# Rotation of the conditioning states: who forms the sums, and in which order the scans and products stand

## The chip, the cores and the metric

One core of a Trainium2 chip runs the whole kernel. The metric is the device time of one execution in microseconds (us). The kernel before took 882.53 us (median of 3 runs, 880.73 to 883.51). The engines are TensorE (PE, matrix products), VectorE (DVE), ScalarE (ACT), GpSimd (POOL) and SyncE (SP, which only issues transfers here). They run side by side and wait for one another by semaphores.

## The reference

The kernel is a small vision tower: patch embedding, a gated linear attention layer with a conditioning branch, a quantised feed-forward layer, softmax attention and a mixture of experts. The change touches only the conditioning branch of the first attention layer. There a projection `p` of the normalised tokens, 128 wide, is taken as 64 pairs, and each pair runs through a recurrence over the 37 tokens of a sequence: the state is turned by a fixed angle and the new pair is added.

```python
p2 = jnp.moveaxis(p.reshape(b, s, bw // 2, 2), 1, 0)
c, sn = (jnp.cos(rot_theta), jnp.sin(rot_theta))
def rot_step(carry, xt):
    s0, s1 = (carry[..., 0], carry[..., 1])
    new = jnp.stack([c * s0 - sn * s1 + xt[..., 0], sn * s0 + c * s1 + xt[..., 1]], axis=-1)
    return (new, new)
_, states = jax.lax.scan(rot_step, init, p2)
cond = _rmsnorm(jnp.moveaxis(states, 0, 1).reshape(b, s, bw), cond_norm_w)
deltas = cond @ delta_W
```

The deltas are then added to the query, key and value projections.

## The kernel before

There are 32 sequences of 37 tokens, 1184 columns in all (`T`), with the features on the 128 partitions. Most stages work in four parts of 296 columns (`CH`); the rotation works in two halves of 592.

The recurrence is computed without a step per token. A state that is turned back by its token's angle obeys a plain running sum. So for each half the kernel does the following (lines 1413 to 1429, VectorE only). It multiplies the two projections (one with even and odd swapped), which lie in PSUM, by tables of cosines and sines: four products, `r1`, `r2`, `r3`, `rp`, for each half. It adds them in pairs (L1423, L1424). It forms two running sums along the tokens with `tensor_tensor_scan` (L1425, L1426), whose first operand `keep_mask` is 0 at the first token of each sequence and 1 elsewhere. It multiplies the running sums by the tables again (L1427, L1428) and adds the two products (L1429); the result in `r1` is the state. After the four products of both halves, the first half goes through all of its seven instructions before the second half starts.

Each finished half increments the semaphore `states`. ScalarE waits for it and squares the half into `rp` (L1101), which increments `csq`. TensorE averages the squares over the partitions with two small products per half (L1891). Between the halves its program has a fixed number of filler products, `keep_clock(fill(("cr", 0)), KEEP["csq"])` with `KEEP["csq"]` = 36 (L1796); they compute nothing that is used, and keep TensorE busy. Then ScalarE takes the square root (L1104), VectorE the reciprocal (L1434), TensorE spreads it over the partitions (L1897), and VectorE scales the states (L1438) and splits them into two halves of precision (L1441). TensorE needs these for the projections that follow.

Before these, TensorE computes the gate projections, whose last product ends while VectorE is in the second half. GpSimd builds constants and masks at the very start (event `masks`) and then waits for the end of this branch (`chl`, L984), after which it builds the decay tables (L991, L995).

Each engine's order is written by hand. `link` increments an engine's own semaphore and, unless `hold=False`, waits for it, so that the next instruction may read what this one wrote. `after(eng, key)` waits until a PSUM bank has been emptied.

Of the kernel before, what the change touches and what calls it, by code (L numbers as in the profile page):

```python
# [7 lines left out]
ALU = mybir.AluOpType  # L8
# [9 lines left out]
NCH = 4  # L18
BC = B // NCH
CH = BC * S  # L20
# [21 lines left out]
for _n, _w in [("cb", 6), ("cw", 24), ("gb", 2), ("dbb", 1), ("opb", 2), ("fcw", 24), ("fcb", 8), ("bq", 2),  # L42
# [16 lines left out]
    + ["wlinh", "wlinl", "xth", "xtl", "condh", "condl", "ctrlh", "ctrll", "dwh", "dwl", "wouth", "woutl", "wqkh",  # L59
       "wqkl", "gwh", "gwl"]  # L60

    + [f"ln{i}_{k}" for i in range(1, 5) for k in ("sq", "rec", "xh", "xl")]

    + ["states", "csq", "crec", "chh", "chl", "dbh", "dbl"]

    + ["conv", "post", "qksq", "qkrec", "kqh", "kql", "vh", "vl"]

# [192 lines left out]
def tower(nc, a, out, probe=None):  # L260
    place = plan_tiles()
    order = list(place)
    with ExitStack() as ctx:
        def sb(name, shape, dt=F32):
            return ctx.enter_context(nc.sbuf_tensor(name, shape, dt))

        def sem(name):
            return ctx.enter_context(nc.semaphore(name))

        ev = {name: sem(name) for name in EVENTS}  # L270
        own = {e: sem("own_" + e) for e in ("act", "dve", "pool")}
# [17 lines left out]
        def who(key):  # L289
            return place[key][1]  # L290

        def nth(key):
            return place[key][2]

        def full(eng, key):

            eng.wait_ge(filled[who(key)], nth(key))
# [3 lines left out]
        xh = sb("xh", [128, 2, TP], F16)  # L301
        xl = sb("xl", [128, 2, TP], F16)
# [14 lines left out]
        def carve(at, *shape, dt=F32, parts=128):  # L317
            n = int(np.prod(shape))
            words = n if dt == F32 else (n + 1) // 2
            assert at + words <= ARENA, (at, words)  # L320
            v = arena[0:parts, at:at + words]
            if dt != F32:
                v = v.bitcast(dt)
            names = "abcde"[:len(shape)]
            return v.rearrange(f"p ({' '.join(names)}) -> p {' '.join(names)}",
                               **{k: s for k, s in zip(names[1:], shape[1:])}) if len(shape) > 1 else v
# [4 lines left out]
        def after(eng, key):  # L331

            eng.wait_ge(emptied[who(key)], nth(key))

        def cols(q, n=CH):
            return slice(q * n, (q + 1) * n)
# [15 lines left out]
        sq = carve(LN_AT + 2368, 2, T)  # L352
# [14 lines left out]
        rp = carve(24640, T)  # L367
        rs_ = carve(25824, T)
        r1 = carve(27008, T)
        r2 = carve(28192, T)  # L370
        r3 = carve(29376, T)
        keep_mask = carve(30560, T)
# [5 lines left out]
        chh = carve(32020, T, dt=F16)  # L378
        chl = carve(32612, T, dt=F16)
# [9 lines left out]
        dbh = carve(13024, T, dt=F16, parts=32)  # L389
        dbl = carve(13616, T, dt=F16, parts=32)  # L390
# [393 lines left out]
        def moe_pe(pe, product, keep_clock):  # L784
# [60 lines left out]
            def rows_out(hf):  # L845
                for n in range(3):
                    pe.wait_ge(ev["summed"], 4 * hf + (2, 4, 4)[n])
                    for t, _, m in half_tiles(0)[2 * n:2 * n + 2]:
                        for c in range(2):
                            at = (t % 2) * D + 128 * c  # L850
                            ins = pe.transpose(banks[ACC[n]][0:m, at:at + 128],
                                               hT[:, c, hf * HALF + 128 * t:hf * HALF + 128 * t + m], ident[:])
                    ins.then_inc(ev["outT"], 1)
# [80 lines left out]
        def _(pool):  # L934
            chain = [0]
# [45 lines left out]
            link(pool.memset(xh[:, :, T:TP], 0.0))  # L981
            pool.memset(xl[:, :, T:TP], 0.0).then_inc(ev["masks"], 1)

            pool.wait_ge(ev["chl"], NCH)  # L984
            pool.wait_ge(ev["dwl"], 1)
            after(pool, ("dbT",))
# [61 lines left out]
        def _(act):  # L1048
            chain = [0]
# [47 lines left out]
                                           bias=sm("gb", c)).then_inc(emptied["act"], 1)  # L1097
            act.activation(warm[:, 4:5], eps[:, 0:1], ACT.Sqrt)
            for h in range(2):
                act.wait_ge(ev["states"], h + 1)  # L1100
                act.activation(rp[:, cols(h, 2 * CH)], r1[:, cols(h, 2 * CH)], ACT.Square).then_inc(ev["csq"], 1)  # L1101
            full(act, ("cv",))

# [69 lines left out]
            for s_ in range(S):  # L1173
# [4 lines left out]
                if WQ_AT <= s_ < WQ_AT + 6:  # L1178
                    i, kind = (s_ - WQ_AT) % 2, (s_ - WQ_AT) // 2
# [122 lines left out]
        def _(dve):  # L1302
            chain = [0]

            def link(ins, hold=True):

                chain[0] += 1
                ins.then_inc(own["dve"], 1)
                if hold:
                    dve.wait_ge(own["dve"], chain[0])  # L1310
# [78 lines left out]
            def small_inputs():  # L1389
# [12 lines left out]
            cosb, sinpb, sinnb = (x.unsqueeze(1).unsqueeze(1).to_broadcast([128, 2, BC, S])  # L1402
                                  for x in (trig[:, 0], sinp, sinn))

            def half(x, h):
                return x[:, cols(h, 2 * CH)].rearrange("p (i b s) -> p i b s", i=2, s=S)

            def pair(i, h):
                b0 = place[("p", i, 2 * h)][0] % 8
                full(dve, ("p", i, 2 * h + 1))  # L1410
                return psum[:, b0:b0 + 2, 0:CH].rearrange("p i (b s) -> p i b s", s=S)

            for h in range(2):
                link(dve.tensor_tensor(half(r1, h), pair(0, h), cosb, ALU.mult), hold=False)
                dve.tensor_tensor(half(r2, h), pair(0, h), sinnb, ALU.mult).then_inc(emptied["dve"], 2)
                link(dve.tensor_tensor(half(r3, h), pair(1, h), sinpb, ALU.mult), hold=False)
                dve.tensor_tensor(half(rp, h), pair(1, h), cosb, ALU.mult).then_inc(emptied["dve"], 2)
            after(dve, ("p", 1, NCH - 1))
            dve.wait_ge(own["dve"], chain[0])
            dve.wait_ge(ev["masks"], 1)  # L1420
            for h in range(2):
                t = cols(h, 2 * CH)
                link(dve.tensor_tensor(r1[:, t], r1[:, t], r3[:, t], ALU.add), hold=False)  # L1423
                link(dve.tensor_tensor(r2[:, t], r2[:, t], rp[:, t], ALU.add))  # L1424
                link(dve.tensor_tensor_scan(r3[:, t], keep_mask[:, t], r1[:, t], 0.0, ALU.mult, ALU.add), hold=False)  # L1425
                link(dve.tensor_tensor_scan(rs_[:, t], keep_mask[:, t], r2[:, t], 0.0, ALU.mult, ALU.add))  # L1426
                link(dve.tensor_tensor(half(r1, h), half(r3, h), cosb, ALU.mult), hold=False)  # L1427
                link(dve.tensor_tensor(half(r2, h), half(rs_, h), sinnb, ALU.mult))  # L1428
                dve.tensor_tensor(r1[:, t], r1[:, t], r2[:, t], ALU.add).then_inc(ev["states"], 1)  # L1429
            dve.wait_ge(ev["states"], 2)  # L1430
            dve.wait_ge(ev["dwh"], 1)
            dve.tensor_tensor(dwl, delta_raw, dwh, ALU.subtract).then_inc(ev["dwl"], 1)
            after(dve, ("cv",))
# [107 lines left out]
            def reduce_o(t):  # L1541
# [3 lines left out]
                                  AX, ALU.add).then_inc(ev["o"], 1)  # L1545

            added_after = [added_by(s_, hi - 1) for s_ in range(S) for _, hi in later_ops(s_)]
            n_ = 0
            for s_ in range(S):
# [137 lines left out]
            for n in range(3):  # L1687
                t = slice(512 * n, min(512 * n + 512, T))
# [89 lines left out]
        def _(pe):  # L1778
# [166 lines left out]
            for key in AORDER:  # L1945
                ps = fill(key)
                if key[0] == "A":
                    _, j, c, n_ = key
                    if (j, c, n_) == (0, 0, 0):
                        keep_clock(ps, KEEP["km"])  # L1950
                    pe.wait_ge(ev["km"], 2 * j + c + 1)
                    for i in range(ASPLIT[n_]):
                        b = ASTART[n_] + i
                        ins = product(ps[0:74, 74 * i:74 * i + 74], kqh[:, c, b].rearrange("p i s -> p (i s)"),
                                      kql[:, c, b].rearrange("p i s -> p (i s)"),
                                      KM[:, c, b].rearrange("p i s -> p (i s)"),
                                      KML[:, c, b].rearrange("p i s -> p (i s)"), True, True)
                else:
                    _, j, n_ = key
                    after(pe, ("A", j, 1, len(ASPLIT) - 1))  # L1960
                    s0, ns = at_group(n_)
                    for x in range(ns):
                        ins = pe.transpose(ps[:, 74 * x:74 * x + 74], ASB[:, j % 2, s0 + x, :], ident[0:74, 0:74])  # L1963
                ins.then_inc(filled[who(key)], 1)
# [317 lines left out]
```

## Time and profile before

| | |
|---|---|
| median of 3 runs | 882.53 us (880.73 to 883.51) |
| profiled execution | 881.1 us, of which 879.4 us are its span |
| TensorE products busy | 793.7 us (90%) |
| VectorE busy | 614.7 us (70%) |
| ScalarE busy | 391.3 us (45%) |
| GpSimd busy | 183.5 us (21%) |
| mean granted clock of TensorE | 0.977 |

The profile is of one execution. The span goes from the first to the last instruction; the time around it is 1.7 us. Busy shares are over the whole span, and a stage can have another limit than the whole. Times in the rows below are us from the start of the span.

### The profile page before, as it was taken

To read this page: it belongs to the slowest core of one execution; us is meant where nothing else is said; L and a number is where in the kernel's file an instruction comes from. 1 tells how busy PE (TensorE), PEld (TensorE's weight loads), DVE (VectorE), ACT (ScalarE), POOL (GpSimd) and SP (SyncE) were. 2 spreads that over 40 slices of the span, in tenths; PEclk is the share of its full clock that TensorE was granted. 3 is DMA by queue.
4 is the path that set the end of the run, shared out by engine and by line. 5 is a ranking of instruction groups with operands and counts; after the bars stand their busy time and mean duration, and the time that the engine had idled before them with its cause. 6 is when DMAs were issued, how large, how long until landed. Compare 5 with 4: busy or idle time off the path is not lost.

```text
span 879.4 us, 19821 instructions
## 1 busy us (share of the span) xinstructions
PE 793.7 (90%) x7700; PEld 586.2 (67%) x7700; DVE 614.7 (70%) x976; ACT 391.3 (45%) x561; POOL 183.5 (21%) x197
## 2 busy tenths in 40 slices
PE   4998978989986988977798998799999999999997
PEld 3665757944543666755487885477777777777775
DVE  5796697678787386898767977767777655545544
ACT  5344764610224143666457965334444432323332
POOL 7000790006999801000402420000000000000000
PEclk9999979999999999999999999799999999999999
DMA  8000000020000000010130001144444322222221
GB/s 310 1 2 1 3 1 3 3 96 1 0 0 1 0 2 1 1 39 1 37 78 14 22 21 38 57 127 158 154 150 154 109 68 57 70 69 69 68 61 51
DMA packets 24073, 46.07 MB, mean 52 GB/s; under 512 B 2605, under 2 KB 10541, under 8 KB 23629
## 3 DMA queue, kind: packets, MB, share of 16 engines
q1 hardware_dynamic: 24013, 45.21, 16.8%
q8 instruction: 45, 0.74, 0.4%
q14 instruction: 15, 0.12, 0.0%
HBM read 41.91 MB, written 1.36 MB: 49 GB/s over the span
## 4 chain that ended last, share of the span: by engine, by line
PE 70%; DVE 21%; ACT 4%; issue 3%; POOL 1%; DMA 1%; SPq 0%; DVEq 0%; ACTq 0%; POOLq 0%
PE psum L1790 11%; PE psum L1791 11%; PE psum L1792 11%; PE psum L1982 6%; PE psum L1992 4%; PE psum L828 4%; PE psum L829 4%; PE psum L830 4%; PE psum L2124 1%; DVE arena L1460 1%; PE psum L2170 1%; DVE arena L1658 1%; PE psum L1963 1%; PE psum L2187 1%; PE psum L2156 1%
## 5 line engine op out<-in xcount | busy, mean ns | idle before, releaser
L1790 PE MATMUL psum<-xh,arena 128*128 128x296 f16 (+1 forms) x664 | 193.3, 291 | 8.3 <-DVE xl L1333 5.0
L1791 PE MATMUL psum<-xl,arena 128*128 128x296 f16 (+1 forms) x664 | 193.2, 291 | 0.0
L1792 PE MATMUL psum<-xh,arena 128*128 128x296 f16 (+1 forms) x664 | 193.2, 291 | 0.0
L697 DVE TENSOR_TENSOR arena<-arena 128x592 f16<-128x592 f32 x68 | 52.7, 775 | 61.1 <-ACT arena L608 60.8
L603 ACT ACTIVATE arena<-psum 128x592 f32<-128x592 f32 x66 | 43.8, 664 | 115.7 <-PE psum L1792 115.7
L1790 PEld LDWEIGHTS psum<-xh,arena 128*128 (+2 forms) x664 | 65.3, 98 | 30.8 <-DVE xl L1333 4.5
L752 DVE TENSOR_TENSOR arena<-psum,arena 128x592 f32<-128x592 f32 x64 | 49.6, 775 | 50.8 <-PE psum L1792 50.6
L828 PE MATMUL psum<-arena 128*128 128x296 f16 x272 | 79.9, 294 | 4.6 <-DVE arena L697 3.8
L608 ACT ACTIVATE arena<-arena 128x592 f16<-128x592 f32 x66 | 46.0, 696 | 77.6 <-DVE arena L691 74.8
L829 PE MATMUL psum<-arena 128*128 128x296 f16 x272 | 79.9, 294 | 0.0
L830 PE MATMUL psum<-arena 128*128 128x296 f16 x272 | 79.8, 293 | 0.0
L1982 PE MATMUL psum<-arena 128*128 128x512 f32 (+1 forms) x160 | 65.8, 550 | 14.2 <-DVE arena L527 14.2
L1792 PEld LDWEIGHTS psum<-xh,arena 128*128 (+2 forms) x664 | 65.4, 98 | 19.1
L1791 PEld LDWEIGHTS psum<-xl,arena 128*128 (+2 forms) x664 | 65.3, 98 | 18.3
L1790 PE MATMUL psum<-arena 128*74 128x74 f16 (+3 forms) x348 | 58.3, 229 | 18.6 <-DVE arena L1343 12.9
L1982 PEld LDWEIGHTS psum<-arena 128*128 128x128 f32 x160 | 30.3, 195 | 46.5 <-issue 28.4
L527 DVE TENSOR_TENSOR arena<-arena,psum 128x320 f32<-128x320 f32 (+7 forms) x67 | 53.9, 805 | 8.4 <-PE psum L1982 8.4
L1012 POOL TENSOR_TENSOR arena<-arena 128x64 f32<-128x64 f32 (+23 forms) x24 | 43.6, 1819 | 72.4 <-ACT arena L1175 55.3
L691 DVE TENSOR_TENSOR arena<-arena 128x592 f32<-128x592 f32 x68 | 52.7, 775 | 8.4 <-ACT arena L603 1.5
L1791 PE MATMUL psum<-arena 128*74 128x74 f16 (+3 forms) x348 | 58.4, 229 | 0.0
L1792 PE MATMUL psum<-arena 128*74 128x74 f16 (+3 forms) x348 | 58.3, 230 | 0.0
L1175 ACT ACTIVATE arena<-arena 128x64 f32<-128x64 f32 x37 | 11.7, 316 | 97.7 <-DVE arena L1560 97.6
(321 smaller groups left out, 1675.3 us busy)
## 6 DMA issues: line engine op xcount, KB each, us to landing
arena<-comb SPq DMA_DIRECT2D x62, 296.0 KB, 3.3
arena<-in_wmoe SPq DMA_DIRECT2D x34, 384.0 KB, 3.0
arena<-in_xt SPq DMA_DIRECT2D x4, 864.0 KB, 9.6
arena<-in_w SPq DMA_DIRECT2D x2, 1024.0 KB, 6.6
arena<-arena SPq DMA_DIRECT2D x6, 187.0 KB
arena<-in_ctrl SPq DMA_DIRECT2D x1, 1056.0 KB, 9.1
out<-arena SPq DMA_DIRECT2D x2, 512.0 KB, 3.1
arena<-in_wlin SPq DMA_DIRECT2D x1, 768.0 KB, 4.4
```

The costliest lines, as they stand in the source:

```text
L527: return eng.tensor_tensor(dst[:, 0:w * HJ * DH].rearrange("p (t j v) -> p t j v", j=HJ, v=DH), a_, u, ALU.mult)
L608: act.activation(ah[:, s_], t1, ACT.Copy).then_inc(ev["ah"], 1)
L691: dve.tensor_tensor(t1, t1, sg, ALU.mult).then_inc(ev["a"], 1)
L697: dve.tensor_tensor(al[:, s_], t1, ah[:, s_], ALU.subtract).then_inc(ev["al"], 1)
L752: dve.tensor_tensor(t1v, up, cb_[:, s_].rearrange("p (c t) -> p c t", c=2), ALU.mult).then_inc(ev["t1"], 1)
L828: pe.matmul(dst, high, ah[:, s_, cols(ch)], start=start, stop=False, skip_group_check=True)
L829: pe.matmul(dst, high, al[:, s_, cols(ch)], start=False, stop=False, skip_group_check=True)
L830: ins = pe.matmul(dst, low, ah[:, s_, cols(ch)], start=False, stop=stop, skip_group_check=True)
L1790: pe.matmul(dst, wh, mh, start=start, stop=False)
L1791: pe.matmul(dst, wh, ml, start=False, stop=False)
L1792: return pe.matmul(dst, wl, mh, start=False, stop=stop)
L1982: pe.matmul(row(g0, g1 - g0), negident, ring[:, n_ % RING, 64 * (g0 - base):64 * (g1 - base)], start=False, stop=s_ + 1 == g0, skip_group_ ...
```

## The change

The six sums of the rotation were all VectorE's. Now GpSimd forms five: four before the scans, and the one that finishes the first half. The one that finishes the second half stays on VectorE. VectorE's order becomes: the eight products from PSUM, the four scans of both halves, then the products back of the first half and of the second. Two semaphores carry this: `rotated`, incremented by VectorE's products, and `rotated_sum`, incremented by GpSimd's sums. ScalarE's first square waits for GpSimd's fifth sum, its second for the only increment of `states`. Two semaphores of another stage that nothing used are gone. TensorE's program, with its 36 fillers, is as before.

```diff
+            for h in range(2):
+                t = cols(h, 2 * CH)
+                pool.wait_ge(ev["rotated"], 2 * h + 2)
+                after(pool, ("p", 1, 2 * h + 1))
+                pool.tensor_tensor(r1[:, t], r1[:, t], r3[:, t], ALU.add).then_inc(ev["rotated_sum"], 1)
+                pool.tensor_tensor(r2[:, t], r2[:, t], rp[:, t], ALU.add).then_inc(ev["rotated_sum"], 1)
+            pool.wait_ge(ev["rotated"], 6)
+            pool.tensor_tensor(r1[:, cols(0, 2 * CH)], r1[:, cols(0, 2 * CH)], r2[:, cols(0, 2 * CH)], ALU.add).then_inc(
+                ev["rotated_sum"], 1)
...
             for h in range(2):
-                act.wait_ge(ev["states"], h + 1)
+                act.wait_ge(*((ev["states"], 1) if h else (ev["rotated_sum"], 5)))
                 act.activation(rp[:, cols(h, 2 * CH)], r1[:, cols(h, 2 * CH)], ACT.Square).then_inc(ev["csq"], 1)
...
             for h in range(2):
-                link(dve.tensor_tensor(half(r1, h), pair(0, h), cosb, ALU.mult), hold=False)
+                dve.tensor_tensor(half(r1, h), pair(0, h), cosb, ALU.mult).then_inc(ev["rotated"], 1)
                 dve.tensor_tensor(half(r2, h), pair(0, h), sinnb, ALU.mult).then_inc(emptied["dve"], 2)
-                link(dve.tensor_tensor(half(r3, h), pair(1, h), sinpb, ALU.mult), hold=False)
+                dve.tensor_tensor(half(r3, h), pair(1, h), sinpb, ALU.mult).then_inc(ev["rotated"], 1)
                 dve.tensor_tensor(half(rp, h), pair(1, h), cosb, ALU.mult).then_inc(emptied["dve"], 2)
-            after(dve, ("p", 1, NCH - 1))
-            dve.wait_ge(own["dve"], chain[0])
             dve.wait_ge(ev["masks"], 1)
             for h in range(2):
                 t = cols(h, 2 * CH)
-                link(dve.tensor_tensor(r1[:, t], r1[:, t], r3[:, t], ALU.add), hold=False)
-                link(dve.tensor_tensor(r2[:, t], r2[:, t], rp[:, t], ALU.add))
+                dve.wait_ge(ev["rotated_sum"], 2 * h + 1)
                 link(dve.tensor_tensor_scan(r3[:, t], keep_mask[:, t], r1[:, t], 0.0, ALU.mult, ALU.add), hold=False)
-                link(dve.tensor_tensor_scan(rs_[:, t], keep_mask[:, t], r2[:, t], 0.0, ALU.mult, ALU.add))
-                link(dve.tensor_tensor(half(r1, h), half(r3, h), cosb, ALU.mult), hold=False)
-                link(dve.tensor_tensor(half(r2, h), half(rs_, h), sinnb, ALU.mult))
-                dve.tensor_tensor(r1[:, t], r1[:, t], r2[:, t], ALU.add).then_inc(ev["states"], 1)
-            dve.wait_ge(ev["states"], 2)
+                dve.wait_ge(ev["rotated_sum"], 2 * h + 2)
+                link(dve.tensor_tensor_scan(rs_[:, t], keep_mask[:, t], r2[:, t], 0.0, ALU.mult, ALU.add), hold=False)
+            dve.wait_ge(own["dve"], chain[0])
+            for h in range(2):
+                t = cols(h, 2 * CH)
+                dve.tensor_tensor(half(r1, h), half(r3, h), cosb, ALU.mult).then_inc(ev["rotated"], 1)
+                dve.tensor_tensor(half(r2, h), half(rs_, h), sinnb, ALU.mult).then_inc(ev["rotated"], 1)
+                if h:
+                    dve.wait_ge(ev["rotated"], 8)
+                    dve.tensor_tensor(r1[:, t], r1[:, t], r2[:, t], ALU.add).then_inc(ev["states"], 1)
+            dve.wait_ge(ev["rotated_sum"], 5)
+            dve.wait_ge(ev["states"], 1)
```

## Rows read from the trace of the kernel before

**Rows 1.** The page: shares of the chain that ended last, by engine.
```profile
PE 70%; DVE 21%; ACT 4%; issue 3%; POOL 1%; DMA 1%; SPq 0%; DVEq 0%; ACTq 0%; POOLq 0%
```

**Rows 2.** The chain of waits from 52 us: start, duration, engine and line.
```profile
52.28 0.79 DVE arena L1416
...
66.66 0.70 ACT arena L1101
67.41 0.72 PE psum L1891 x4
```

**Rows 3.** VectorE's timeline, 50 to 67: start, duration, line, operation, shapes.
```profile
50.08 0.76 DVE L1417 TENSOR_TENSOR arena<-psum,arena 128x592 f32<-128x592 f32 x1
50.77 0.76 DVE L1414 TENSOR_TENSOR arena<-psum,arena 128x592 f32<-128x592 f32 x1
...
52.98 0.76 DVE L1417 TENSOR_TENSOR arena<-psum,arena 128x592 f32<-128x592 f32 x1
53.77 0.78 DVE L1423 TENSOR_TENSOR arena<-arena 128x592 f32<-128x592 f32 x1
...
55.27 1.39 DVE L1425 TENSOR_TENSOR_SCAN arena<-arena 128x592 f32<-128x592 f32 x1
56.58 1.36 DVE L1426 TENSOR_TENSOR_SCAN arena<-arena 128x592 f32<-128x592 f32 x1
...
65.85 0.77 DVE L1429 TENSOR_TENSOR arena<-arena 128x592 f32<-128x592 f32 x1
```

**Rows 4.** ScalarE's timeline at 60 us; in brackets the idle before and its releaser.
```profile
60.28 0.70 ACT L1101 ACTIVATE arena<-arena 128x592 f32<-128x592 f32 x1 [0.69 <-DVE arena L1429]
```

**Rows 5.** TensorE's timeline, 60 to 68 us.
```profile
60.26 0.29 PE L1792 MATMUL psum<-xh,arena 128*128 128x296 f16 x1
61.12 0.69 PE L1891 MATMUL psum<-arena,mean_ones 128*32 128x296 f32 x4 [0.57 <-ACT arena L1101]
61.75 4.82 PE L1796 MATMUL psum<-arena 128*128 128x296 bf16 x36
67.41 0.69 PE L1891 MATMUL psum<-arena,mean_ones 128*32 128x296 f32 x4 [0.84 <-ACT arena L1101]
```

**Rows 6.** GpSimd's groups, shapes apart: busy us and mean ns, then idle before.
```profile
L1043 POOL TENSOR_TENSOR arena<-arena 101x592 f16<-101x592 f32 x16 | 20.3, 1268 | 66.2 <-ACT arena L1292 66.2
...
L995 POOL TENSOR_TENSOR arena<-arena 128x444 f32<-128x444 f32 x4 | 3.7, 932 | 0.0
...
L1012 POOL TENSOR_TENSOR arena<-arena 128x640 f32<-128x640 f32 x1 | 1.5, 1529 | 0.0
...
L527 POOL TENSOR_TENSOR arena<-arena 128x576 f32<-128x576 f32 x1 | 1.2, 1216 | 0.0
```

**Rows 7.** GpSimd's timeline, 121 to 126 us.
```profile
121.98 0.48 POOL L995 TENSOR_TENSOR arena<-arena 128x169 f32<-128x169 f32 x1
...
123.08 0.94 POOL L995 TENSOR_TENSOR arena<-arena 128x444 f32<-128x444 f32 x1
124.09 1.51 POOL L995 TENSOR_TENSOR arena<-arena 128x169 f32<-128x169 f32 x1
```

**Rows 8.** VectorE's timeline, 120 to 126 us.
```profile
120.29 1.32 DVE L1473 TENSOR_TENSOR arena<-arena 128x1184 f16<-128x1184 f32 x1
...
122.65 0.45 DVE L1488 TENSOR_TENSOR arena<-arena,psum 128x296 f32<-128x296 f32 x1
123.13 2.13 DVE L1473 TENSOR_TENSOR arena<-arena 128x1184 f16<-128x1184 f32 x1
```

**Rows 9.** TensorE: an idle in its timeline; stretches (length, busy, granted clock, DMA).
```profile
188.70 1.99 PE L1982 MATMUL psum<-arena 128*128 128x512 f32 x3 [3.65 <-DVE arena L527]
...
73.50:73.60 0.10, 0.10 (x2) 0.88 0.00 0
76.90:77.00 0.10, 0.10 (x2) 0.56 0.00 0
189.60:189.70 0.10, 0.10 (x2) 0.64 0.00 0
193.00:193.10 0.10, 0.10 (x2) 0.80 0.00 0
```

More of the change, by code:

```diff
@@ L60 @@
        "wqkl", "gwh", "gwl"]
-    + [f"ln{i}_{k}" for i in range(1, 5) for k in ("sq", "rec", "xh", "xl")]
-    + ["states", "csq", "crec", "chh", "chl", "dbh", "dbl"]
+    + [f"ln{i}_{k}" for i in range(1, 5) for k in (("sq", "rec") if i == 2 else ("sq", "rec", "xh", "xl"))]
+    + ["rotated", "rotated_sum", "states", "csq", "crec", "chh", "chl", "dbh", "dbl"]
     + ["conv", "post", "qksq", "qkrec", "kqh", "kql", "vh", "vl"]
```

## The prediction

> **What bounds the kernel now.** I read the chain of waits first. TensorE has 70% of the chain and VectorE 21% [rows 1], but a share over the whole span does not price this edit; the stage does. In the stage of the rotation the chain is all VectorE, from the product at 52.28 us to the end of the last sum; then it goes through ScalarE's square at 66.66 and TensorE's small products at 67.41 [rows 2]. VectorE's timeline gives the durations there [rows 3]: pieces of 592 columns take 0.76 to 0.78 us, and start 0.69 us apart with no wait between them (50.08, 50.77) or 0.79 with one (52.98, 53.77); a scan takes 1.39 or 1.36 us and the next starts after 1.31.
>
> TensorE's timeline [rows 5] is the view that decides. Its last gate product ends at 60.26 + 0.29 = 60.55. The squares of the first half come from ScalarE at 60.28 + 0.70 = 60.98 [rows 4], its products of the first half start at 61.12, and behind them in its queue stand 36 filler products that keep its clock, written in the program between the two halves: 61.75 to 66.57. The second half starts at 67.41, after an idle of 0.84. So today the fillers fit between the halves, because the first half's states are ready 6.4 us before the second's. They are not conditional: whenever the first half starts, the second cannot start before 0.63 + 4.82 us have passed, plus the little gap that a change of product costs, in all about 5.5.
>
> **The change part by part.** VectorE loses five of six sums, nominally 5 x 0.69 to 0.79, or some 3.7 us. The order also changes: all four scans now come before any product back, and the sum that finishes the first half is GpSimd's fifth. Call the four scans S1 to S4 (first half S1, S2), GpSimd's sums P1 to P5, the products back Q1 to Q4.
>
> P1 and P2. GpSimd has had nothing to do since its masks were done. Its wait ends with the last product of the first half, 50.08 + 0.76 = 50.84. No row has a dense sum of 592 in f32 on GpSimd; the nearest are 444 elements at 0.93 us, 576 at 1.216, 592 with f16 out at 1.268, and 640 in another line at 1.529 [rows 6]. I take 1.25, nearest to the 576 and the 592, and keep 0.95 and 1.5 as ends. P1 and P2 run 50.9 to 53.4, beside VectorE's products that read PSUM and one table. That costs nothing: a GpSimd piece of 169 elements beside VectorE's PSUM products takes 0.48 [rows 7], and those keep their 0.45 [rows 8]. If that cover were wrong, S1 would start up to 1.2 us late.
>
> S1 to S4 with P3 and P4. Here the two engines are not independent. At 123.08 GpSimd starts a piece of 0.94, ending 124.02; VectorE's piece with two SBUF inputs starts at 123.13 and takes 2.13 us, against 1.32 for the same shape at 120.29. It ends at 125.26, 1.24 after GpSimd let go. The next GpSimd piece, 169 elements, starts at 124.09 and takes 1.51 instead of 0.48: it ends at 125.60, 0.34 after VectorE [rows 7, 8]. So each waits for the whole of the other's instruction; a waiting VectorE piece then needs its duration less 0.08, a waiting GpSimd piece its duration less 0.14. A scan reads two SBUF tensors (the keep mask and the sums), as does a product back. No row shows a scan beside GpSimd: the bounds are no conflict, and the full one. I take the full one.
>
> The Trainium skill, GPSIMD Engine Reference, Key points, says that GpSimd shares its SBUF interfaces with VectorE and contends with VectorE instructions that have two SBUF inputs. A scan has two, so by that rule it belongs with the piece at 123.13, and the sum below stands; without it the sum would be the smaller one that I give as a rival.
>
> The sum, with conflict. S1 starts at 52.98 + 0.69 = 53.67 and has the port; P3 may start only at 53.8, when the last PSUM product is done, and waits. S1 ends 55.03; P3 ends 55.03 + 1.11 = 56.14; S2 ends 56.14 + 1.28 = 57.42; P4 ends 58.53; S3 ends 59.81; S4 follows with nothing of GpSimd's in between and ends 61.1. (If GpSimd did not get in between S1 and S2, S3 would have to wait for P3 instead, and the total would be the same.) Q1 and Q2 end at 61.15 + 0.69 + 0.76 = 62.6. P5 needs Q2, but Q3 is already running until 63.3, so P5 ends at 63.3 + 1.11 = 64.4. ScalarE's square: 64.43 to 65.13. TensorE starts the first half 0.14 later, as it does now [rows 4, 5], at 65.27; its fillers run 65.90 to 70.72; the second half starts at 70.74. Before: 67.41. That is **+3.3 us**. VectorE meanwhile ends Q4 at 65.1 and the last sum at 65.9; the second half's squares are there at 66.6, four microseconds before they are wanted. So the states are done slightly earlier than now (65.9 against 65.85 + 0.78 = 66.6 [rows 3]), and it buys nothing: what is late next is the filler queue. P3, P4 and P5 each carry the GpSimd price, so its ends move the sum by -0.9 and +0.8.
>
> The clock. TensorE would idle from 60.55 to 65.27, 4.7 us, where it now idles 0.57. After its idle of 3.65 us at 188.70 the granted clock fell from 2.4 to 1.2 GHz at 189.63 and came back at 193.04 [rows 9]: the granted shares in the edge slices (0.64 and 0.80) place the two edges. Those 3.4 us at the lower level cost 1.7 us of work. A spell like that at about 65 would fall into the fillers, which take twice as long in it. Bounds: 0, and 3.4 for two spells in a row; I take **+1.7**.
>
> The rest moves as a block. The square root, the reciprocal, the row broadcast and TensorE's projections hang on the second half and shift with it. VectorE's subtraction for the delta weights still hides under the squares. The two removed semaphores and the two new ones have no instruction of cost. Nothing downstream starts without this chain, so nothing absorbs the shift.
>
> The sum is 3.3 + 1.7 = 5.0 us. The profiled execution took 881.1 us (span 879.4); that gives 886.1. The median of the three runs is 882.53, 1.4 above the profiled one, so the forecast on its scale is 887.5.
>
> **The rivals.** (a) Conflict, but no extra clock spell, or one later spell less: the change costs 3.3, 885.8. For it: shorter idles at this stage leave the clock alone. Against: the idle becomes eight times as long.
>
> (b) Scans and GpSimd do not conflict. S4 ends at 53.67 + 3 x 1.31 + 1.36 = 58.96, Q2 at 60.4, P5 at 61.75, the squares at 62.5, TensorE starts at 62.6 and the second half at 68.1: +0.7, 883.2; with a clock spell +2.4, 884.9. For it: no row shows a scan beside GpSimd. Against: the piece at 123.13.
>
> (c) Not slower. The mechanism: as (b), and the fillers, which then run without the present gap of 0.84 before the second half, spare TensorE the clock spell that now begins at 73.58 and ends at 76.99 (edge slices 0.88 and 0.56 [rows 9]), just as it needs its rate for the projections. That gives back 1.7: -1.0, 881.5. It decides in favour as soon as the first half reaches TensorE before 61.95 (67.41 less 5.46), or before 63.6 if the spell goes. With the conflict it comes at 65.3, so even without that spell the sum is above zero. To beat 0.3% it would need the fillers gone from between the halves, and they are not.
>
> **How the numbers follow.** Forecast 0.45 (4.1 to 5.9 us by the GpSimd price; 886.6 to 888.5), (a) 0.25, (b) 0.16, (c) 0.08, other clock spells in stages that start 5 us later 0.06. A difference within 0.3%, 2.65 us either way, cannot be told from none here. All of the forecast, 0.20 of (a) and 0.05 of (b) and the rest lie above it: slower 0.70. Faster needs (c) with a second spell gone: 0.03. Same 0.27. The range must reach (b) at 883.2 and stop above the forecast with half a spell and a dear GpSimd more: 882.8 to 890.2.
>
> **What would show it.** Right: GpSimd's third and fourth sums take over 2 us each, or the scans do; the fourth scan ends near 61; TensorE idles over 4 us from 60.5; the first half's products start near 65.3 and the second's come straight behind the 36 fillers with no wait for ScalarE; ScalarE's second square ends well before. A granted clock of 1.2 GHz within the fillers shows the last term. Wrong: scans 1.31 apart beside GpSimd's sums (then (b)); a GpSimd sum far from 1.25 us in P1 and P2; a wait for the squares behind the fillers, which would mean that the second half and not the filler queue is late.

## The result: slower by 0.7%, and the profile after

The changed kernel took 889.29 us in the median of 7 runs (884.88 to 892.63), the kernel before 882.89 us beside it. The ratio is 1.007, with a 95% interval of 1.0046 to 1.0093: 4 to 8 us slower. In a second set (12 runs) the medians were 887.18 and 883.39 us and the ratio 1.0059 (1.0031 to 1.0087). A ratio is worked out from all runs of both kernels and need not be that of the two medians, so both are given below. The profiled execution took 884.88 us, the fastest of the first seven, so its span of 883.2 us shows less than the median does; the stage itself has to be read in the trace.

The shares of the chain are nearly those of [rows 1]: TensorE 70%, VectorE 20% for 21%, GpSimd 2% for 1%.

VectorE's timeline of the changed kernel, to be read against [rows 3]. The last product from PSUM starts at 52.96, as before (52.98):

```profile
53.64 1.44 DVE L1432 TENSOR_TENSOR_SCAN arena<-arena 128x592 f32<-128x592 f32 x1
55.01 2.55 DVE L1434 TENSOR_TENSOR_SCAN arena<-arena 128x592 f32<-128x592 f32 x1
57.48 2.56 DVE L1432 TENSOR_TENSOR_SCAN arena<-arena 128x592 f32<-128x592 f32 x1
59.96 1.36 DVE L1434 TENSOR_TENSOR_SCAN arena<-arena 128x592 f32<-128x592 f32 x1
61.36 0.77 DVE L1438 TENSOR_TENSOR arena<-arena 128x592 f32<-128x592 f32 x1
...
62.73 0.77 DVE L1438 TENSOR_TENSOR arena<-arena 128x592 f32<-128x592 f32 x1
63.42 2.00 DVE L1439 TENSOR_TENSOR arena<-arena 128x592 f32<-128x592 f32 x1
65.45 0.78 DVE L1442 TENSOR_TENSOR arena<-arena 128x592 f32<-128x592 f32 x1
```

GpSimd's timeline, the five sums:

```profile
50.98 1.45 POOL L988 TENSOR_TENSOR arena<-arena 128x592 f32<-128x592 f32 x1 [31.22 <-DVE arena L1427]
52.39 1.44 POOL L989 TENSOR_TENSOR arena<-arena 128x592 f32<-128x592 f32 x1
53.87 2.45 POOL L988 TENSOR_TENSOR arena<-arena 128x592 f32<-128x592 f32 x1
56.27 2.52 POOL L989 TENSOR_TENSOR arena<-arena 128x592 f32<-128x592 f32 x1
62.90 1.89 POOL L991 TENSOR_TENSOR arena<-arena 128x592 f32<-128x592 f32 x1 [4.10 <-DVE arena L1439]
```

The two views interlock: GpSimd and VectorE take turns. Whichever engine is at work is said to have the port, as in the prediction; no run looks behind that word. The first scan has the port until about 55.1; the third sum, issued at 53.87, ends at 56.32. The second scan, alone 1.36, takes 2.55; the fourth sum waits for it and ends at 58.79; and the third scan takes 2.56. The same happens with the fifth sum (1.89) and the last product back (2.00 in place of 0.77). Beside the products from PSUM a sum takes 1.45.

ScalarE's squares, against [rows 4], and TensorE's timeline, against [rows 5]:

```profile
64.82 0.70 ACT L1111 ACTIVATE arena<-arena 128x592 f32<-128x592 f32 x1 [5.25 <-POOL arena L991]
66.27 0.70 ACT L1111 ACTIVATE arena<-arena 128x592 f32<-128x592 f32 x1 [0.75 <-DVE arena L1442]
```
```profile
60.24 0.29 PE L1806 MATMUL psum<-xh,arena 128*128 128x296 f16 x1
65.66 1.20 PE L1905 MATMUL psum<-arena,mean_ones 128*32 128x296 f32 x4 [5.13 <-ACT arena L1111]
66.80 6.44 PE L1810 MATMUL psum<-arena 128*128 128x296 bf16 x36
73.17 0.69 PE L1905 MATMUL psum<-arena,mean_ones 128*32 128x296 f32 x4
```

The second half's squares are there at 66.97. TensorE uses them at 73.17, because the 36 fillers stand in front, and it reached these late and at the low clock. Before, that row was at 67.41. The chain, which in [rows 2] went from VectorE through ScalarE's second square to TensorE, now passes through the fillers:

```profile
64.82 0.71 ACT arena L1111
65.53 0.14 issue
65.66 1.20 PE psum L1905 x4
66.87 6.37 PE psum L1810 x36
73.24 0.65 PE psum L1905 x4
```

The granted clock at the two edges of the low spell (stretch; length, busy, granted clock, DMA), against [rows 9]:

```profile
63.30:63.40 0.10, 0.00 (x0) 0.98 0.00 0
...
70.20:70.30 0.10, 0.10 (x2) 0.88 0.00 0
```

It falls to 1.2 GHz at 63.4, 2.9 us into the idle that began at 60.53, and returns to 2.4 GHz at 70.2. That is 6.8 us, twice the 3.4 us of the spell at 189.63 in [rows 9]. TensorE had work in 4.5 us of it, which costs 2.3 us.

Executions differ by up to 1.6 us in when this stage begins, so from here on I measure the second half from the start of the last product from PSUM: before 67.41 - 52.98 = 14.43 us, changed 73.17 - 52.96 = 20.21, a loss of 5.8.

GpSimd's first clear of the decay tables comes 6.7 us later than before; the attention weights' turn at 391 us only 3.7 later. The rows of the kernel before:

```profile
92.39 0.36 POOL L988 MEMSET arena<- 128x148 f32 x1 [72.51 <-ACT arena L1124]
...
391.39 2.39 PE L2032 MATMUL psum<-ident,arena 128*128 128x128 f32 x10 [3.88 <-DVE arena L1658]
```

and of the changed kernel:

```profile
99.05 0.36 POOL L998 MEMSET arena<- 128x148 f32 x1 [34.26 <-ACT arena L1134]
...
395.13 2.40 PE L2046 MATMUL psum<-ident,arena 128*128 128x128 f32 x10 [3.88 <-DVE arena L1672]
```

In between the kernel before has the low spell at 189.63 to 193.04 [rows 9], and the changed kernel's profile has none there: 1.7 of the 3 us. It has one from 315.9 to 319.4 that the kernel before lacks. So what is left of a delay at the end of one execution also hangs on where such spells fall; whether that is a rule in the times is taken up below.

### The profile page after: what moved, and what is told of

Read it like the earlier page. It is cut to its first block, busy times and chain, and to the rows that moved or that the text cites. A ratio compares the mean times of both kernels' runs of the same rounds, so it can differ in the third digit from the quotient of the medians.

```text
span 883.2 us, 19823 instructions
## 1 busy us (share of the span) xinstructions
PE 797.3 (90%) x7700; PEld 588.3 (67%) x7700; DVE 615.3 (70%) x971; ACT 391.2 (44%) x561; POOL 192.7 (22%) x202
## 3 DMA queue, kind: packets, MB, share of 16 engines
HBM read 41.91 MB, written 1.36 MB: 49 GB/s over the span
## 4 chain that ended last, share of the span: by engine, by line
PE 70%; DVE 20%; ACT 4%; issue 3%; POOL 2%; DMA 1%; SPq 0%; DVEq 0%; ACTq 0%; POOLq 0%
PE psum L1804 11%; PE psum L1805 11%; PE psum L1806 11%; PE psum L1996 6%; PE psum L2006 4%; PE psum L828 4%; PE psum L829 4%; PE psum L830 4%; PE psum L2138 1%; DVE arena L1474 1%; PE psum L2184 1%; DVE arena L1672 1%; PE psum L1977 1%; PE psum L2201 1%; PE psum L2170 1%
## 5 line engine op out<-in xcount | busy, mean ns | idle before, releaser
L697 DVE TENSOR_TENSOR arena<-arena 128x592 f16<-128x592 f32 x68 | 52.7, 775 | 61.1 <-ACT arena L608 60.9
L1996 PE MATMUL psum<-arena 128*128 128x512 f32 (+1 forms) x160 | 63.9, 537 | 12.5 <-DVE arena L527 12.5
L1804 PEld LDWEIGHTS psum<-arena 128*74 128x74 f16 (+2 forms) x348 | 38.4, 116 | 23.2 <-issue 14.8
```

Source lines behind the costliest of these rows:

```text
L697: dve.tensor_tensor(al[:, s_], t1, ah[:, s_], ALU.subtract).then_inc(ev["al"], 1)
L1804: pe.matmul(dst, wh, mh, start=start, stop=False)
L1996: pe.matmul(row(g0, g1 - g0), negident, ring[:, n_ % RING, 64 * (g0 - base):64 * (g1 - base)], start=False, stop=s_ + 1 == g0, skip_group_ ...
```

## The experiments

Theory: three terms. The port and the new order delay the first half; the fillers, which stand behind the first half in TensorE's queue, then delay the second; the idle before them costs the clock. Rivals: GpSimd or the new order is slow in itself; all of it is the clock; all of it is the queue.

**The fillers in front of the first half.** In TensorE's program of the changed kernel:

```diff
-                if q == 2:
+                if q == 0:
                     keep_clock(fill(("cr", 0)), KEEP["csq"])
```

> The changed kernel with its 36 fillers moved from between the halves to in front of the first half's products on TensorE. Theory (the fillers stand behind a first half that now comes late, and the idle of 5 us costs the clock): the fillers run at 60.6 to 65.4 at 2.4 GHz, the first half's products start near 65.7, the second's near 67.1 (before: 67.41, changed kernel: 73.17), no spell of 1.2 GHz at 63 to 71; the time is within 1.5 us of the kernel before, some 6 under the changed one. Rival (the sums on GpSimd and the new order on VectorE themselves make it slow): the second half's products stay near 73 or the time stays 4 us or more above the kernel before.

Measured: 882.87 us against 883.3, ratio 1.0002 (0.9977 to 1.0028). TensorE's timeline:

```profile
61.27 4.81 PE L1810 MATMUL psum<-arena 128*128 128x296 bf16 x36
66.48 0.69 PE L1905 MATMUL psum<-arena,mean_ones 128*32 128x296 f32 x4 [0.40 <-ACT arena L1111]
67.92 0.69 PE L1905 MATMUL psum<-arena,mean_ones 128*32 128x296 f32 x4 [0.75 <-ACT arena L1111]
```

This execution ran 0.9 us late from the start (last product at 53.86): the second half is at 14.06, 0.37 under the kernel before, and it waits for ScalarE again. With GpSimd's five sums, the stretched scans and the new order all kept, the whole loss is gone. What the change cost came through the place of the fillers; what it gained in the stage was 0.4 us.

**No fillers between the halves** (the changed kernel with `"csq": 0` for 36).

> The changed kernel with no fillers at all between the halves (36 to 0). Theory: the first half starts at 65.7 as in the changed kernel, after the same idle of 5.1 us and with the clock at 1.2 GHz, the second near 67.1; the 16 fillers and the small products behind it run at the low clock, so it pays 1 to 2 us of the clock but not the 4.8 of the fillers: 1 to 3 us above the kernel before. Rival: the fillers' only effect is on the clock and without them later stages lose more than 5 us: no better than the changed kernel.

Measured: 885.08 us against 883.3, ratio 1.002 (0.9998 to 1.0042), +1.8 us. (One run of the twelve took 2751 us, and why is not known. The median counts it and would be 884.82 without it; the ratio leaves it out.) TensorE's timeline:

```profile
66.49 1.20 PE L1905 MATMUL psum<-arena,mean_ones 128*32 128x296 f32 x4 [5.13 <-ACT arena L1111]
67.94 1.20 PE L1905 MATMUL psum<-arena,mean_ones 128*32 128x296 f32 x4 [0.24 <-ACT arena L1111]
69.07 3.64 PE L1810 MATMUL psum<-arena 128*128 128x296 bf16 x16
```

The second half starts on time (67.94 - 53.79 = 14.15), but at 1.2 GHz: its products take 1.20 for 0.69 and the 16 fillers behind them 3.64 for 2.24. The size is as expected, though the interval's lower end touches no change.

**Fillers in both places.** The changed kernel with `if q in (0, 2):`, 72 fillers in all.

> The changed kernel with 36 fillers in front of the first half as well, those between the halves kept. It parts the queue from the clock: the theory says that the clock stays at 2.4 GHz from 60 to 71, the first half's products start where they do in the changed kernel, and the second's 0.63 + 4.84 later, that is 3.6 us after the place of the kernel before (14.43 us after the last product from PSUM; here 18.0) and 2.1 us earlier than in the changed kernel (20.2). Time: +3 to +4 us against the kernel before. Rival (all of the loss is the clock): back to the kernel before, 14.4. Rival (all of it is the queue): no better than the changed kernel, 20.2.

Measured: 887.84 us against 883.39, ratio 1.0044 (1.0024 to 1.0064), +3.9 us. TensorE's timeline:

```profile
60.47 4.81 PE L1810 MATMUL psum<-arena 128*128 128x296 bf16 x36
65.68 0.69 PE L1905 MATMUL psum<-arena,mean_ones 128*32 128x296 f32 x4 [0.40 <-ACT arena L1111]
66.31 4.82 PE L1810 MATMUL psum<-arena 128*128 128x296 bf16 x36
71.06 0.69 PE L1905 MATMUL psum<-arena,mean_ones 128*32 128x296 f32 x4
```

The second half is at 71.06 - 53.06 = 18.0, as expected to the tenth. So of the 5.8 us, 3.6 are the queue and 2.2 the clock. Both rivals that name one cause fall by the place of the second half; the times alone (2.1 to 5.7 us here, 2.7 to 7.7 for the changed kernel in the same set) would not part this kernel from the changed one.

**More fillers in the kernel before:** 66, and after that 96, in place of 36 (`"csq": 66`, `"csq": 96`). Its sums, scans and order are untouched.

> The kernel before with 66 fillers between the halves in place of 36, nothing else. Theory: the queue of fillers is what the second half waits for once it is longer than the gap between the halves: 30 x 0.134 = 4.0 us more, less the idle of 0.84 that is there: second half at 70.6 in place of 67.41, time +3.2 us. Rival (the fillers pay for themselves by the clock): less than +1.5 us.

> The kernel before with 96 fillers between the halves in place of 36. The dose of 66 gave a second half 3.0 us late but a time only +0.2% (0 to 0.47%), too near to both readings. Theory: 60 x 0.134 less 0.84 = 7.2 us late at the second half, and the time follows: +5.5 to +8 us. Rival (later stages absorb a delay of this stage, through the clock or otherwise): second half 7.2 late, time under +4.

The rows of the second half, first with 66, then with 96:

```profile
70.09 0.69 PE L1891 MATMUL psum<-arena,mean_ones 128*32 128x296 f32 x4
```
```profile
74.54 0.69 PE L1891 MATMUL psum<-arena,mean_ones 128*32 128x296 f32 x4
```

With 66 it starts 17.4 after the last product (3.0 late), with 96 21.3 (6.9 late). The times: with 66, 883.99 us against 883.3, ratio 1.0023 (1.0 to 1.0047), that is +2.0 us (0 to 4.1); with 96, 891.69 against 883.39, ratio 1.0093 (1.0061 to 1.0126), +8.2 us. In the trace the first dose does what the theory says, but its time does not tell the readings apart: the medians differ by 0.7 us, which is what the rival expected, and the ratio lies between the two. The second dose does: a delay of 6.9 us in this stage is not absorbed later.

**Four more GpSimd sums in the kernel before.** They read the keep mask and write to a spare place; nothing uses them. (The wait that lets the last two start also stands on VectorE, which costs its first scan 0.1 us.)

```diff
+            for x in range(4):
+                if x == 0:
+                    after(pool, ("p", 1, 1))
+                elif x == 2:
+                    pool.wait_ge(ev["extra_go"], 1)
+                pool.tensor_tensor(spare[:, x], keep_mask[:, cols(0, 2 * CH)], keep_mask[:, cols(1, 2 * CH)],
+                                   ALU.add).then_inc(ev["extra"], 1)
```

> The kernel before, its own sums all on VectorE, with four GpSimd sums of 128x592 more whose output nothing reads: two start beside VectorE's products from PSUM, two beside the first half's scans. Theory (a VectorE instruction with two SBUF inputs and a GpSimd sum exclude each other, products from PSUM do not): the first two take 1.45 us and the products keep 0.76; the last two take about 2.5, the scan beside them 2.5 in place of 1.36, and the states of both halves come some 2.4 us later. Rival (in the changed kernel the scans were late by their waits on the sums, not by the port): all four take 1.45 and both scans keep 1.36 to 1.44.

GpSimd's timeline and then VectorE's:

```profile
51.17 1.44 POOL L990 TENSOR_TENSOR arena<-arena 128x592 f32<-128x592 f32 x1 [31.41 <-DVE arena L1426]
52.57 1.46 POOL L990 TENSOR_TENSOR arena<-arena 128x592 f32<-128x592 f32 x1
55.55 1.44 POOL L990 TENSOR_TENSOR arena<-arena 128x592 f32<-128x592 f32 x1 [1.52 <-DVE arena L1433]
56.95 2.53 POOL L990 TENSOR_TENSOR arena<-arena 128x592 f32<-128x592 f32 x1
```
```profile
52.52 0.77 DVE L1425 TENSOR_TENSOR arena<-psum,arena 128x592 f32<-128x592 f32 x1
...
55.58 2.67 DVE L1440 TENSOR_TENSOR_SCAN arena<-arena 128x592 f32<-128x592 f32 x1
58.17 2.56 DVE L1441 TENSOR_TENSOR_SCAN arena<-arena 128x592 f32<-128x592 f32 x1
```

Nothing in these scans depends on those sums, and yet each is stretched, by 1.2 to 1.3 us. Beside PSUM products neither engine feels the other. One detail differs from what was expected: the third sum, which came 0.03 us ahead of the scan, took its own 1.44, and it was the scan that waited; who comes first goes first. The second half starts at 17.67, 3.2 us late, and its 36 fillers take 5.91 us for 4.82, since a low spell falls into them. There is one execution, 881.94 us; a single time says nothing here, and the stage is what was asked.

**The second half's sums back on VectorE,** between the scans of the two halves:

```diff
+                if h:
+                    ...
+                    link(dve.tensor_tensor(r1[:, t], r1[:, t], r3[:, t], ALU.add), hold=False)
+                    link(dve.tensor_tensor(r2[:, t], r2[:, t], rp[:, t], ALU.add))
```

> The changed kernel with the second half's two first sums back on VectorE, between the scans of the two halves; its order and the other three GpSimd sums stay. Theory: both scans beside which the sums stood go back from 2.56 to 1.36 us, the two sums take 0.69 and 0.8 there, so that the products back start 0.8 to 0.9 us earlier, and with them the first half's squares; the fillers and the clock spell stay, so the second half starts near 19.3 us after the last product from PSUM (changed kernel: 20.2, before: 14.43), and the time stays 4 us or more above the kernel before. Rival (the shared port is the main loss): most of the 5.8 us comes back.

Measured: 887.14 us against 882.31, ratio 1.0057 (1.0032 to 1.0081). VectorE's timeline, then TensorE's:

```profile
54.88 1.36 DVE L1441 TENSOR_TENSOR_SCAN arena<-arena 128x592 f32<-128x592 f32 x1
56.16 0.74 DVE L1434 TENSOR_TENSOR arena<-arena 128x592 f32<-128x592 f32 x1
...
60.33 0.78 DVE L1445 TENSOR_TENSOR arena<-arena 128x592 f32<-128x592 f32 x1
```
```profile
64.64 1.20 PE L1912 MATMUL psum<-arena,mean_ones 128*32 128x296 f32 x4 [4.23 <-ACT arena L1111]
65.77 6.84 PE L1817 MATMUL psum<-arena 128*128 128x296 bf16 x36
72.54 0.69 PE L1912 MATMUL psum<-arena,mean_ones 128*32 128x296 f32 x4
```

The scans are back at 1.36 and the products back start 0.9 us earlier, but the second half only 0.5 (19.71), since more of the fillers falls into the spell (6.84 for 6.44). So who forms these two sums decides 0.5 of the 5.8 us. This does not price the port alone: of the 2.4 us that the two scans get back, the two sums on VectorE take 1.5 again, and the fifth sum still shares the port (2.00 for the last product back). What is left is mostly the order, by an estimate from these rows: between the first half's scans and its products back stand the second half's two sums and two scans, 56.16 to 60.33, some 4.2 us. No run has the new order with all sums on VectorE, so this share is not measured by itself.

**Only the first two sums on GpSimd, in the order of before.** From the kernel before; the two sums stand beside products from PSUM, and the first half is still finished first.

```diff
+            pool.tensor_tensor(r1[:, t], r1[:, t], r3[:, t], ALU.add).then_inc(ev["rotated_sum"], 1)
+            pool.tensor_tensor(r2[:, t], r2[:, t], rp[:, t], ALU.add).then_inc(ev["rotated_sum"], 1)
...
             for h in range(2):
                 t = cols(h, 2 * CH)
-                link(dve.tensor_tensor(r1[:, t], r1[:, t], r3[:, t], ALU.add), hold=False)
-                link(dve.tensor_tensor(r2[:, t], r2[:, t], rp[:, t], ALU.add))
+                if h:
+                    ...
+                else:
+                    dve.wait_ge(ev["rotated_sum"], 1)
```

> The kernel before with only the first half's two first sums on GpSimd, where VectorE reads PSUM, and VectorE's old order of halves. Theory (what is slow is the order and the shared port, not GpSimd's help as such): the sums take 1.45 us each beside the products, the first scan starts at 53.7 in place of 55.3, the first half's squares wait for nothing, the second half reaches TensorE at 65.9 to 66.1 in place of 67.41: -1.4 us against the kernel before. Rival (any sum on GpSimd costs as much as it saves): no gain, first scan at 55 or later.

> The kernel before with only the first half's two first sums on GpSimd, once more, because its interval of 0.995 to 1.0002 just held no change. Theory: second half 12.9 us after the last product from PSUM in place of 14.43, time 1 to 3 us under the kernel before. Rival: the first result was luck of the later clock spells, and the time is the same within 0.5 us.

TensorE's timeline in the second set:

```profile
60.66 0.69 PE L1902 MATMUL psum<-arena,mean_ones 128*32 128x296 f32 x4
61.28 4.82 PE L1807 MATMUL psum<-arena 128*128 128x296 bf16 x36
66.04 0.69 PE L1902 MATMUL psum<-arena,mean_ones 128*32 128x296 f32 x4
```

In both profiles the second half starts at 12.89, 1.54 us under the kernel before, with fillers and squares done together: nothing idles. The times: 880.18 against 883.3, ratio 0.9976 (0.995 to 1.0002), and 882.16 against 882.31, ratio 0.9987 (0.9968 to 1.0006). Both ratios point down, by 2.1 and 1.1 us, and each interval holds no change. The second pair of medians differs by only 0.15 us, which is what the rival expected. The gain in the stage is shown; that the whole kernel is faster is not.

In both traces one more thing is gone: the low spell that the kernel before has from 73.58 to 76.99 [rows 9]. That is the mechanism that the prediction's rival (c) named. A stretch of the second trace (length; TensorE busy, granted clock, DMA):

```profile
74.00:76.00 2.00, 2.00 (x17) 1.00 0.02 4
```

**The changed kernel again.**

> The changed kernel itself once more, beside the others on the same chip: +5 to +7.5 us against the kernel before; its second half starts 20.2 us after the last product from PSUM. If the stage's loss is given back later as a rule, as the first profile (+3.8) would have it, the median is under +4.5.

Its second half is at 20.24, in the trace the same as the first time. The time leaves the question open. The ratio of 1.0059 (1.0031 to 1.0087) is +5.2 us (2.7 to 7.7), near the 5.8 of the stage. But the medians, 887.18 against 883.39, differ by 3.8, and a median under +4.5 was named beforehand as the sign that later stages give back. Against a rule speak all the sets together. By the ratio, the time differs by at most 1.4 us from the delay of the second half, to either side: the changed kernel has 5.8 us in the stage and 6.2 and 5.2 in time, fillers in both places 3.6 and 3.9, 66 fillers 3.0 and 2.0, 96 fillers 6.9 and 8.2. (The run without fillers is no such pair, since its loss falls behind the start of the second half.) That part of a delay is given back is not excluded.

## Why the prediction was right

It said 887.5 us, from +3.3 for port and queue and +1.7 for the clock; the median was 889.29, +6.4. That is above the 886.6 to 888.5 that it gave its likeliest case, and inside its whole range, up to 890.2. The mechanism was right at each step, and both terms were too small. Step by step:

The conflict. The likeliest case had the scans and the sums exclude each other, on the ground of one piece at 123.13 [rows 7, 8] and none with a scan. The runs show it for scans. The times named were 57.4 for the end of the second scan (57.56 measured), 59.8 for the third (60.04), 61.1 for the fourth (61.32). Rival (b), no conflict, fell with the extra sums.

GpSimd's price. This term was too small: 1.25 taken, 1.45 measured, inside the bounds of 0.95 and 1.5. None of the rows it was worked out from [rows 6] was the same instruction, and the 576 elements at 1.216 misled. The same view of the kernel before has another row of 576, of the line that also has the 640 at 1.529:

```profile
L1012 POOL TENSOR_TENSOR arena<-arena 128x576 f32<-128x576 f32 x1 | 1.4, 1407 | 0.3 <-DVE arena L1544 0.3
```

Between these two, 592 elements come to 1.44, which is what was measured. The price made the fifth sum end at 64.79 in place of 64.4, and TensorE start at 65.66 in place of 65.27. The third, fourth and fifth sum ended 1.24, 1.23 and 1.29 us after the VectorE instruction that they waited for; the prediction had 1.11.

The queue. +3.3 predicted, 3.6 measured with fillers in both places; the difference is mostly GpSimd's price. That the VectorE work saved buys nothing was right: the second half's squares lay ready for 6.2 us.

The clock. +1.7 predicted, one spell; 2.2 measured. The spell began within the idle and lasted 6.8 us, double, of which 4.5 had work in it. The bounds of 0 and 3.4 held it. That 1.7 came so near is in part luck: the prediction took the length of 3.4 us from another idle and had the engine at work all through it, and of the real spell, twice as long, 2.3 us fell where there was no work. Rival (a), without it, is the kernel with fillers in both places.

The rest. That nothing later absorbs the shift is borne out for a large one: the dose of 96 fillers gave 6.9 us in the stage and 8.2 (5.4 to 11.1) in time. For 3 to 6 us the times do not decide it. Rival (c) needed the first half at TensorE before 61.95; it came at 65.66. Its other half, that the later spell at 73.58 would go, was not borne out either: the changed kernel has one from 80.5 to 83.9. It did go in the kernel with two sums on GpSimd, whose first half is early.

## What to carry to other kernels

Filler products that keep the clock are work with a place in the queue: before something in front of them is delayed, work out when they would end, and move them to where the idle now is. A sum given to GpSimd was free where VectorE read PSUM, and cost VectorE most of its length (1.2 of 1.45 us) where VectorE had two SBUF inputs. When a first half feeds a fixed block of another engine's work that ends after the last half is ready, the time of the first half matters, not that of the last.

## What the runs showed of the hardware

A dense f32 sum of 128x592 takes 1.45 us on GpSimd, more than the 576 elements at 1.216 and the 592 at 1.268 of other lines would suggest. The exclusion between it and a VectorE instruction with two SBUF inputs works both ways and is of whole instructions: 1.36 becomes 2.56 and 1.45 becomes 2.5. A spell of 1.2 GHz can begin while TensorE has nothing to do, 2.9 us into an idle, and then last 6.8 us. The point and the length vary: without fillers it began 3.9 us into the idle and lasted 6.8, with the four extra sums it began 3.1 us in, just as work resumed, and lasted 3.4. The times of one and the same kernel spread over 8 to 10 us here (879.2 to 887.1 before, 883.7 to 893.7 changed), as much as the effects in question; positions in the stage repeat to 0.05 us (20.21 and 20.24; 12.89 twice).
